# Neighbour-decay layer: additions of two units in one pass and one mask pass over two tiles

## The reference, cut to what matters

```python
# x: 4096 x 64 fp32, adj: 4096 x 4096 fp32 of zeros and ones (about one in 256 is a one)
h = relu(layernorm(x))
support = h @ weight                              # 4096 x 64
mask = (adj != 0)
rank = cumsum(mask, axis=1); deg = rank[:, -1:]
k = minimum(deg, 100)
pos = rank - (deg - k)
w = mask * where(pos > 0, 0.5 ** (k - pos), 0)    # each neighbour weighs half of the next one to its right
out = x + w @ support + bias
```

## Time and profile before

| | before |
|---|---|
| median of 3 runs | 216.44 us (216.24 to 216.45) |
| the profiled execution | 216.8 us, of which the span of its instructions is 214.2 us |
| TensorE matmul busy | 196.7 us, 92% of the span, 2784 matmuls |
| TensorE weight load busy | 188.0 us |
| VectorE busy | 196.8 us, 92%, 239 instructions |
| ScalarE busy | 160.6 us, 75% |
| GpSimd busy | 29.1 us, 14% |
| granted TensorE clock | full speed in all 40 slices |
| moved by DMA | 36.09 MB, the queues busy until about 167 us |

### The profile page before, as it was taken

How to read it: one execution, slowest core, us unless ns; L and a number is a source line. 1 busy time by engine, 2 the same in 40 slices (tenths; PEclk the granted TensorE clock), 3 DMA queues, 4 the chain that set the end, 5 groups by cost and what they waited for, 6 DMA issues and landing times.

```text
span 214.2 us, 6505 instructions
## 1 busy us (share of the span) xinstructions
PE 196.7 (92%) x2784; PEld 188.0 (88%) x2784; DVE 196.8 (92%) x239; ACT 160.6 (75%) x303; POOL 29.1 (14%) x53
## 2 busy tenths in 40 slices
PE   0369979999999999999999999999999999999993
PEld 0269657997898999999999999999999999999993
DVE  1999979797979999999999999989999999998893
ACT  2442996786786988778778778789978989998720
POOL 7800000000010404010004110500000000000000
PEclk9999999999999999999999999999999999999999
DMA  6999999999999999999999999999998000000001
GB/s 203 204 217 220 216 211 216 216 219 212 218 213 221 210 218 216 213 220 216 211 222 212 217 218 215 216 217 218 221 209 174 8 12 3 12 15 3 17 0 43
DMA packets 7677, 36.09 MB, mean 168 GB/s; under 512 B 1506, under 2 KB 3298, under 8 KB 3554
## 3 DMA queue, kind: packets, MB, share of 16 engines
q0 software_dynamic: 4608, 33.56, 75.1%
q1 hardware_dynamic: 2882, 2.10, 3.8%
q10 hardware_dynamic: 160, 0.03, 0.1%
HBM read 68.19 MB, written 1.05 MB: 323 GB/s over the span
## 4 chain that ended last, share of the span: by engine, by line
PE 81%; DVE 7%; ACT 6%; DMA 2%; issue 1%; SPq 0%; DVEq 0%
PE acc L633 40%; PE chain L626 25%; PE chain L624 14%; ACT powers L313 3%; ACT support L296 3%; DMA x_sb<-in_x 2%; DVE masks L358 2%; PE chain L612 2%; DVE sq_sum L460 1%; DVE powers L455 1%; DVE later L399 1%; DVE row_sum L451 1%; DVE part L364 1%; DVE acc L481 0%; DVE sums L364 0%
## 5 line engine op out<-in xcount | busy, mean ns | idle before, releaser
L313 ACT ACTIVATE powers<-chain 128x512 int16<-128x512 f32 (+1 forms) x279 | 148.7, 573 | 33.6 <-PE chain L626 31.4
L633 PE MATMUL acc<-support,powers 128*128 128x192 bf16 x1024 | 159.5, 246 | 1.3 <-ACT powers L313 1.2
L626 PE MATMUL chain<-diag_own,masks 128*128 128x128 bf16 x608 | 107.1, 219 | 0.1
L624 PE MATMUL chain<-diag_past,masks 128*128 128x128 bf16 x568 | 102.2, 219 | 2.1 <-ACT powers L313 1.5
L633 PEld LDWEIGHTS acc<-support,powers 128*128 128x128 bf16 x1024 | 95.9, 98 | 4.3 <-ACT powers L313 2.4
L358 DVE TENSOR_SCALAR masks<-adj_b 128x4096 uint8<-128x4096 bf16 x32 | 72.6, 2281 | 5.0 <-DMA adj_b<-in_adj 5.0
L624 PEld LDWEIGHTS chain<-diag_past,masks 128*128 128x128 fp8e3 x568 | 55.5, 99 | 5.3 <-ACT powers L313 3.9
L626 PE MATMUL chain<-diag_step,masks 128*128 128x128 bf16 x416 | 60.1, 219 | 0.0
L626 PEld LDWEIGHTS chain<-diag_own,masks 128*128 128x128 fp8e3 x608 | 59.7, 99 | 0.3 <-issue 0.3
L626 PEld LDWEIGHTS chain<-diag_step,masks 128*128 128x128 fp8e3 x416 | 39.5, 99 | 0.0
L242 POOL DMA_DIRECT2D adj_b<-in_adj x32 | 24.5, 767 | 108.9 <-DVE masks L358 107.7
(11 more groups left out here) (52 smaller groups left out, 66.3 us busy)
## 6 DMA issues: line engine op xcount, KB each, us to landing
adj_b<-in_adj POOLq DMA_DIRECT2D x32, 1024.0 KB, 35.0
x_sb<-in_x SPq DMA_DIRECT2D x2, 512.0 KB, 4.5
out<-x_sb SPq DMA_DIRECT2D x14, 64.0 KB, 5.4
out<-x_sb SPq DMA_DIRECT2D x4, 32.0 KB, 9.5
w<-in_L_gnn_weight ACTq DMA_DIRECT2D x2, 16.0 KB, 9.1
bias<-in_L_gnn_bias SPq DMA_DIRECT2D x1, 0.2 KB
```

The costliest lines, as they stand in the source:

```text
L313: nc.scalar.activation(powers[:, c, b, cols].bitcast(i16), chain[c][:, cols], ACT.Relu, bias=(MAX_NEIGH + 1) * STEP).then_inc(powers_ready ...
L624: nc.tensor.matmul(chain[c][:, at:at + P], column(n, t + 1), diag_past[:, :], start=False, stop=False, skip_group_check=True)
L626: return nc.tensor.matmul(chain[c][:, at:at + P], column(n, t), diag_own[:, :] if marked else diag_step[:, :], start=False, stop=True, ski ...
L633: return nc.tensor.matmul(acc[u % ACCS][:, k * 3 * D:(k + 1) * 3 * D], powers[:, u % FLIGHT, s + 1 if k < MARKS[u] else s, at:at + P], sup ...
```

## The change

Four pairs of neighbouring units (4+5, 6+7, 8+9, 14+15; `PAIRED`) are added up together: each of the three additions handles both `acc` banks in one instruction of 128x256, at the slots of the unit that ends later, and SyncE stores the rows of both in one DMA. The wait of `before_products` is on the set that held the bank. For the units 11 to 16 (`TWINS`) one instruction masks both tiles, 128x8192, in the slot in which the second tile was masked before; the planes of both tiles lie in one another, so `halve_1` and `halve_2` work on one run of double length. The buffers of `adj_b` are shifted by one so that the two tiles lie side by side. In the order, units 1 and 2 start one slot later, unit 17 too, and seven entries of `LAGS` differ: unit 5 10 to 9, unit 8 9 to 11, unit 10 10 to 11, unit 11 12 to 11, unit 13 11 to 12, unit 14 11 to 10, unit 16 9 to 10 (and with the starts, the products of the units 1, 2 and 17 move by one slot).

```diff
-    STARTS = [0, 5, 6, 14, 23, 27, 34, 40, 45, 51, 57, 63, 68, 74, 80, 85, 91, 97]
-    LAGS = [8, 5, 9, 10, 9, 10, 9, 8, 9, 8, 10, 12, 11, 11, 11, 10, 9, 8]
+    STARTS = [0, 6, 7, 14, 23, 27, 34, 40, 45, 51, 57, 63, 68, 74, 80, 85, 91, 98]
+    LAGS = [8, 5, 9, 10, 9, 9, 9, 8, 11, 8, 11, 11, 11, 12, 10, 10, 10, 8]
...
+    PAIRED = (4, 6, 8, 14)
+
+    TWINS = (11, 12, 13, 14, 15, 16)
...
+    def added_with(u):
+
+        return u - 1 if u - 1 in PAIRED else u
+
+    def sets_until(u):
+
+        f = added_with(u)
+        return sum(added_with(v) == v for v in range(f % ACCS, f + 1, ACCS))
+
+    def units_of(f):
+        return [f, f + 1] if f in PAIRED else [f]
...
-        acc = [pb(f"acc{a}", [P, 512], fp32) for a in range(ACCS)]
+        accs = pb("accs", [P, ACCS, 512], fp32)
+        acc = [accs[:, a, :] for a in range(ACCS)]
...
-                pool.dma_start(adj_b[:, n % LOADS, :], adj_t[n]).then_inc(adj_loaded[n % LOADS], 16)
+                pool.dma_start(adj_b[:, (n + SHIFT) % LOADS, :], adj_t[n]).then_inc(adj_loaded[n % LOADS], 16)
...
+            def mask_both(u):
+
+                n = FIRST[u]
+                for k in range(2):
+                    dve.wait_ge(adj_loaded[(n + k) % LOADS], 16 * ((n + k) // LOADS + 1))
+                if n >= RING:
+                    v = UNIT_OF[n + 1 - RING]
+                    dve.wait_ge(chain_ready[v % FLIGHT], taken_until(v) + TAKEN[v])
+                    v = UNIT_OF[n - RING]
+                    dve.wait_ge(chain_ready[v % FLIGHT], taken_until(v) + TAKEN[v])
+                at = (n + SHIFT) % LOADS
+                two = adj_b[:, at:at + 2, :].rearrange("q k (r e) -> q (k r) e", e=2)\
+                    .rearrange("q (r j) e -> q j r e", r=2 * RUNS_OF[n])
+                nc.vector.tensor_scalar(planes_of_both(u), two, 0.0, 1.0,
+                                        ALU.not_equal, ALU.mult).then_inc(mask_ready, 2)
...
+            def parts_of(u, s):
+                n, k = len(units_of(u)), SIZES[u]
+                return accs[:, u % ACCS:u % ACCS + n, 0:k * 3 * D].rearrange("q n (k s d) -> q n k s d", s=3, d=D)[:, :, :, s, :]
 
             def add_low(u):
-                dve.wait_ge(acc_ready[u % ACCS], u // ACCS + 1)
-                dve.wait_ge(xb_ready, 1 + (FIRST[u] + SIZES[u] > T // 4))
-                nc.vector.tensor_tensor(sum_a[:, u % ACCS, 0:SIZES[u], :], parts_of(u)[:, :, 2, :], rows_of(u),
+                for v in units_of(u):
+                    dve.wait_ge(acc_ready[v % ACCS], v // ACCS + 1)
+                dve.wait_ge(xb_ready, 1 + (FIRST[u] + len(units_of(u)) * SIZES[u] > T // 4))
+                nc.vector.tensor_tensor(rows_of(sum_a, u), parts_of(u, 2), rows_of(x_sb, u),
                                         ALU.add).then_inc(low_added[u % ACCS], 1)
...
-                    if u >= 3 and to == 8 and FIRST[u] > 3:
+                    if u >= 3 and to == 8 and FIRST[u] > 3 and u not in TWINS:
                         mask(FIRST[u])
                     if u >= 3 and to == 7 and SIZES[u] > 1:
-                        mask(FIRST[u] + 1)
+                        if u in TWINS:
+                            mask_both(u)
+                        else:
+                            mask(FIRST[u] + 1)
...
-                    done = STARTS[u] + LAGS[u] + STEPS[u]
+                    if added_with(u) != u:
+                        continue
+                    done = max(STARTS[v] + LAGS[v] + STEPS[v] for v in units_of(u))
...
-                    pe.wait_ge(rows_done[u % ACCS], u // ACCS)
+                    pe.wait_ge(rows_done[added_with(u - ACCS) % ACCS], sets_until(u - ACCS))
```

More of the change, by code:

```diff
@@ L92, in batches_until @@
         return sum(STEPS[v] // BATCH[v] for v in range(u % FLIGHT, u, FLIGHT) if MARKS[v] < SIZES[v])
+    def added_with(u):
[5 more added lines that the diff above has]
+        return [f, f + 1] if f in PAIRED else [f]
     def halved_until(u):
         return sum(2 if CHAINS[v] == 2 else 1 for v in range(u))
+    SETS = [u for u in range(NU) if added_with(u) == u]
     SLOTS = max(STARTS[u] + LAGS[u] + STEPS[u] for u in range(NU))
@@ L206, in gnn_decay_kernel, with planes_of_both @@
         RUNS_OF = [CHAINS[UNIT_OF[n]] * P for n in range(NT)]
+        def planes_of_both(u):
+            at = (FIRST[u] + SHIFT) % RING
+            return masks[:, at:at + 2, :].rearrange("q k (r e) -> q (k r) e", e=2)\
+                .rearrange("q (j r) e -> q j r e", r=2 * CHAINS[u] * P)
         def planes_of(n):
-            return masks[:, (n + SHIFT) % RING, :].rearrange("q (j r e) -> q j r e", r=RUNS_OF[n], e=2)
+            u, at = UNIT_OF[n], (n + SHIFT) % RING
+            if u in TWINS:
+                both = planes_of_both(u)
+                k = n - FIRST[u]
+                return both[:, :, k * RUNS_OF[n]:(k + 1) * RUNS_OF[n], :]
+            return masks[:, at, :].rearrange("q (j r e) -> q j r e", r=RUNS_OF[n], e=2)
         def in_planes(tensor, n):
@@ L228, in _ @@
             sp.dma_start(bias_1[:, :], bias.rearrange("(a d) -> a d", a=1)).then_inc(bias_loaded, 16)
-            for u in range(NU):
-                sp.wait_ge(rows_done[u % ACCS], u // ACCS + 1)
-                rows = slice(FIRST[u], FIRST[u] + SIZES[u])
+            for u in SETS:
+                sp.wait_ge(rows_done[u % ACCS], sets_until(u))
+                rows = slice(FIRST[u], FIRST[u] + sum(SIZES[v] for v in units_of(u)))
                 sp.dma_start(out_t[:, rows, :], x_sb[:, rows, :]).then_inc(stored, 16)
-            sp.wait_ge(stored, 16 * NU)
+            sp.wait_ge(stored, 16 * len(SETS))
         @block.gpsimd
@@ L374, in halve_1 @@
                 dve.wait_ge(mask_ready, n + k)
-                halve(u, masks[:, at:at + k, :].bitcast(u16), words(part1, u, STEPS[u] // 4), halved)
+                ins = masks[:, at:at + k, :].bitcast(u16)
+                if u in TWINS:
+                    ins = ins.rearrange("q k w -> q (k w)").unsqueeze(1)
+                halve(u, ins, words(part1, u, STEPS[u] // 4), halved)
             def halve_2(u):
@@ L425, in differ, with rows_of @@
                 nc.vector.tensor_tensor(before, before, after, ALU.subtract).then_inc(weights_ready[c], 1)
-            def parts_of(u):
-                return acc[u % ACCS][:, 0:SIZES[u] * 3 * D].rearrange("q (k s d) -> q k s d", s=3, d=D)
-            def rows_of(u):
-                return x_sb[:, FIRST[u]:FIRST[u] + SIZES[u], :]
+            def rows_of(tensor, u):
+                n, k = len(units_of(u)), SIZES[u]
+                if tensor is x_sb:
+                    return x_sb[:, FIRST[u]:FIRST[u] + n * k, :].rearrange("q (n k) d -> q n k d", n=n)
+                return tensor[:, u % ACCS:u % ACCS + n, 0:k, :]
@@ L444, in add_high @@
             def add_high(u):
-                dve.wait_ge(middle_added[u % ACCS], u // ACCS + 1)
-                nc.vector.tensor_tensor(rows_of(u), parts_of(u)[:, :, 0, :], sum_b[:, u % ACCS, 0:SIZES[u], :],
+                dve.wait_ge(middle_added[u % ACCS], sets_until(u))
+                nc.vector.tensor_tensor(rows_of(x_sb, u), parts_of(u, 0), rows_of(sum_b, u),
                                         ALU.add).then_inc(rows_done[u % ACCS], 1)
```

19 lines of the change are left out of this document (14 added, 5 removed).

## The result

The kernel after takes 217.90 us (median of 6 runs, 217.20 to 218.34) against 216.29 us (6 runs, 215.96 to 216.45) of the kernel before, run beside it: ratio 1.0058, with a 95% interval of 1.0038 to 1.0078. The change makes the kernel slower by about 0.6% (the medians themselves differ by 1.61 us, 0.74%), more than the 0.2% that a measurement can tell, and the time lies above the range that was forecast.

A forecast was written before the change was run, and what follows sets the result against it. TensorE's matmuls were taken as the bound from 71 us on; 0 ahead of slot 36, 0 from VectorE, 0 to 0.1 at slot 79 and an unchanged tail left the 216.44 us median at a forecast 216.4, range 215.4 to 217.2.

The forecast's parts named there:

- The long mask runs at the rate of the short one: Two-tile masks of units 11 to 16: about 4.4 us each; rival of half rate, about 235 us, chance 0.02.
- no tile makes a long mask wait: Two-tile masks from about 113.1 us: both tiles landed in time, with a possible covered wait of some 0.3 us.
- The two loads that a long mask frees: Tile loads 27 to 31: issued at most 2.2 us later, behind the long mask, costed at nothing.
- The rival of set 8+9: First product of slot 79, 154.58 us: its bank comes free late, giving 216.7 to 217.6 us; chance 0.14.
- VectorE's busy time: Whole kernel: 18 VectorE instructions fewer, busy time about 1 to 2.5 us lower, nothing of it on the path after 71 us.
- Base 10: Base of unit 10 on TensorE, 114.10 us: room behind its scans shrinks from 1.0 to 0.36 us, no wait.
- The sum for a removed instruction: VectorE: 0.15 - 0.08 = 0.07 us for each instruction removed, 1.3 us for 18.
- the tail: End of the kernel: unit 16's three additions and last store stay as before, costed at nothing.
- the term for the late instructions: TensorE's "issue" waits after slot 36, 1.0 us: they might thin out, giving 215.5 us; chance 0.22.
- the same in the other direction: TensorE after slot 36: one or two more late instructions of 0.5 us, giving 216.9 to 217.4 us; chance 0.06.
- Sum at slot 36: 0: TensorE ahead of slot 36, about 71.17 us: later starts of units 1 and 2 shift its beginning by 0 us.

The follow-up runs named there:

- the second one: Trace of a repeat of the changed kernel with no edit, six more runs: 218.32 us, ratio 1.0090 to the kernel before.
- the order with units 1 and 2 back: Changed kernel without sets and long masks, new starts and lags kept, but units 1 and 2 at slots 5 and 6: 216.67 us, ratio 1.0006.

## Why the prediction was wrong

**Right.** TensorE's matmuls are the bound from slot 36 on and their sum did not move. The long mask runs at the rate of the short one, an addition of 128x256 takes 0.42 us, and no tile makes a long mask wait: the first of them starts at 113.20 us, forecast 113.1. The two loads that a long mask frees are issued in 1.05 us together, behind it, so no load stood in its way. The rival of set 8+9 did not come. These are VectorE's lines from that `floor` on:

```profile
142.78 0.67 DVE L469 TENSOR_SCALAR powers<-powers 128x2048 int16<-128x2048 int16 x1
...
144.69 4.42 DVE L402 TENSOR_SCALAR masks<-adj_b 128x8192 uint8<-128x8192 bf16 x1
149.15 1.23 DVE L408 TENSOR_TENSOR part<-masks 128x2048 uint16<-128x2048 uint16 x1
...
153.62 0.42 DVE L506 TENSOR_TENSOR x_sb<-accs,sum_b 128x256 f32<-128x256 f32 x1
```

From 142.78 to 154.04 us are 11.26 us, forecast 11.1 to 11.3; slot 79 starts at 154.51, so the bank is free 0.47 us ahead, more than the 0 to 0.15 foreseen, as the `floor` came 0.5 us earlier than the 143.27 of the prediction.

**Close.** VectorE's busy time fell by 0.8 us, where 1 to 2.5 were given. Base 10 was to keep 0.36 us of room and waited 0.15 us (the wait of 0.2 for L453 above): its scans ended at 113.29 us, 0.2 us later than before, and base 10 came at 113.34. It costs 0.15 us of the profiled execution. The sum for a removed instruction has a slip, which changes nothing: its own overlap of 0.07 us gives 0.15 - 0.07 = 0.08, and 1.4 us for 18; measured are 0.04 each.

**Wrong, first step: the tail, "the last store waits for unit 16's additions, as before", costed at nothing.** The additions were indeed as before, to 0.04 us. The landing behind them was not: +0.59 us. The prediction counted what the removed instructions do and not where they stand in the code: 22 fewer (18 operations and four waits) move each later block boundary of VectorE by 22 places. There is no cover for anything that comes behind the last addition, so all of it is time.

**Wrong, second step: the term for the late instructions.** The prediction saw that the stops of the earlier trace rows are instructions that come late "beside full DMA queues", and took the order of the work as neutral to them; it gave 0.22 to fewer of them, and 0.06 to "the same in the other direction", 216.9 to 217.4. The runs put about 0.75 us on the new starts, of which these stops and the clock are the two parts that a trace shows. No row of before has the sign, but one row bore on it: a stop of 0.50 us in the middle of a group is a block that came late, and a shift of any kind deals these places anew. The range had to reach as far up for it as it reached down.

**Wrong, third step: "Sum at slot 36: 0".** It was +0.39 us in the trace of the result, 0.42 in the second one and 0.39 in the order with units 1 and 2 back. In the first it is the stop of 0.77 us at 53.05 us; in the other two base 5 waited for tile 8 and its scans, 0.68 and 0.58 us, where the prediction had 0.17 as fixed by the tiles. In the long stretch behind it the profiled execution got 0.35 us back: from slot 36 to the end of the last product it took 139.32 us, where the kernel before took 139.67.

**A term that was not there: the clock.** The prediction took TensorE's clock as given, since the profile of before has it at full speed throughout. In 17 of 59 runs with the later starts it was not, for up to 1.7 us by one stretch of 3.41 us at 1.2 GHz. This touches the kernel after in one run of twelve, so it is not why its time lay outside.

**What stays open.** The traces of the kernel after show the 0.6 us of the tail, but only 0.04 us up to there, while its other runs are mostly slower than the profiled ones (217.45 us is the lowest but one of the first six, and 217.46 the lowest of the second six). That their additional time is in TensorE's stops is an inference: the stops change from run to run, the order with few of them is level, and satisfied waits in TensorE's list alone take the loss away, in its runs at full clock above all. No trace shows the stops of those runs. Nor is it shown why this start of units 1 and 2 meets the tile loads worse, if it does, or why it goes with the low clock.

## What to carry to other kernels

When an edit changes how many instructions an engine has, look where that engine's code packets fall before and after, above all against whatever comes last. A packet of code in the last store went with 0.6 us here, and 22 one-element memsets took both away. Look at the mean clock of every run beside its time: it told part of a difference that no wait explained. In a kernel with full DMA queues, an effect under 0.5% of an edit that no engine's wait explains should be tried again with the code shifted by a few instructions, before it is believed. And work saved on an engine beside the bound was worth nothing here (0.8 us of it): give it a forecast of zero, and spend the range on the tail and on the fetches.

## What the runs showed of the hardware that was not expected

- A code packet of 8 KB that starts between a store's issue and its landing goes with a later landing. In the kernel after with units 1 and 2 back, the last of the store's packets ends at 213.53 us, only 0.11 us later than the 213.42 of the kernel before, but the landing is seen 0.78 us behind it, where it was 0.38. The delay is in the report of the landing more than in the data. The last stores of the four traces with such a packet took 2.11 to 2.17 us, those without 1.57 or 1.58; stores in mid-work with a packet that starts up to 1.05 us after their issue took 2.3 to 3.1 us.
- TensorE's code comes in packets of 16 KB, 22 of them in this kernel. Beside the tile loads they start up to 7.1 us after the block before began, and the engine goes on about 2.4 us after the start, so a block of some 8 us hides them only just.
- The order of the work goes with TensorE's clock: with units 1 and 2 one slot later, 17 of 59 runs have a mean clock of 0.992 or less, against none of 71. In the one trace of this, the clock is at 1.2 GHz from 31.68 to 35.09 us.
- A one-element memset costs VectorE 15 ns (22 in 0.33 us, from 142.73 to 143.07 us), so a list can be shifted at nearly no cost; with the same 22 at the head a tile landed 1.0 us later.
